# An adaLN transformer block in split float32 on one core: order of the first statistics, rotations, feed-forward rows and last products

## The chip, the core and the metric

One core of a Trainium2 chip. The metric is the device time of one execution in microseconds. The kernel before takes 795.87 us (median of 3 runs, 794.94 to 796.75).

## The reference, cut to what matters

Two batches of 512 tokens of width 512 go through attention with 32 query heads on 8 key heads (rotary embedding, causal mask) and then a gated feed-forward. Both are modulated by six vectors per batch, made from c by one product.

```python
mod = (_silu(L0_c) @ L0_wmod).reshape(L0_c.shape[0], 6, 1, -1)
sa, ca, ga, sb, cb, gb = (mod[:, 0], mod[:, 1], mod[:, 2], mod[:, 3], mod[:, 4], mod[:, 5])
ga = (2 * (ga >= 0) - 1) * jnp.maximum(jnp.abs(ga), 0.25)
gb = (2 * (gb >= 0) - 1) * jnp.maximum(jnp.abs(gb), 0.25)
h = _layernorm(x, axis=-1) * (1 + ca) + sa
x = x + ga * _L0_attn_ref(h, L0_attn_wq, L0_attn_wk, L0_attn_wv, L0_attn_wo)
h = _layernorm(x, axis=-1) * (1 + cb) + sb
x = x + gb * _L0_ffn_ref(h, L0_ffn_w12, L0_ffn_b12, L0_ffn_w3, L0_ffn_b3)
```

In the attention q, k and v are projections of h, q and k are rotated (`q * cos + rotate_half(q) * sin`), and the masked softmax of their product weighs v. The feed-forward is `silu(x1) * x2` of one projection, then a second projection.

## The kernel before, in words

Every float32 product on TensorE is made of three products of rounded parts: each operand has a high part (rounded to fp32r, made by ACT, `split_hi`, L1162) and a low part (operand minus high part, made mostly by POOL, `split_lo`, L1412). A product of 128x512 over 512 rows is thus twelve matmuls.

Five instruction streams are written out by hand, one for each engine, and meet only through semaphores. Each engine takes its stream in order, so a wait holds all that stands behind it. SP issues the DMAs.

*Prologue.* The first batch's rows are normalised on DVE: `bn_stats` (L1064), `norm_scale` (Newton steps, L1011), four `tensor_scalar` (L1067, `x_normed[0]`). PE turns them (`turn_x`), ACT modulates them (`modulate_x`, L1228), DVE and ACT make high and low parts (L1073, L1075, `h_lo[0]`). PE makes k, the four heads q of the first group, v, and between them `modulation_rows(3)` and `(4)` (eight matmuls each). A projection is rotated by `first_rotation(n)` on DVE (three `tensor_tensor`, L823 to L825, `roped`), summed by `rotated_sum` on POOL (L1438, `rope_sum`), split by `rotated_high` on ACT (`rope_hi`) and `rotated_low` on POOL (`rope_lo`). rope_tmp has two buffers, so rotation n waits for `rope_lo` n - 1. In between stand the second batch's statistics (L1087), its `norm_scale(1, 2)`, ACT's normalisation (L1360), `turn_x(1)`, `modulate_x(1, k)` and DVE's `h_low(k)`. POOL waits for `norm_ready` before rotation 1's sum. The first scores need `rope_lo` 5 and `h_ready[1]`.

*Groups.* Eight groups g of eight slots s follow, a slot being one tile of 128 query rows of one batch (r = s % 4; tile order 0, 3, 1, 2) for the four heads of a key head. In a slot PE makes scores (into four `s_bank`s), the next query head (`slot_query`, q_bank), at r = 0 the next k and at r = 2 v (x_bank), the product with v of slot s - 3 (`attend`, o_bank) and the output product of slot s - 4 (`project_out`, out_bank). DVE takes maxima, ACT exponents and normalises, DVE turns 32x32 blocks (`turn_blocks`, L878), SP writes these to DRAM (`blocks_to_dram`, L342) and reads them back by keys (`blocks_to_keys`, L350). ACT and POOL split them in slot s + 2. POOL also splits weights: wq in slots 1 to 4 of a group, wk in slot 2, wv in slot 4, wo in slot 4.

Twelve feed-forward row blocks u (`F_SLOTS`, L41: slots 7, 11, 15, ... 51, r = 3) are prepared beside: loaded in the slot before (`load_f_rows`, which waits for the stores of u - 1, u = 0 for the gates' stores), turned on DVE at the end of slot m (`turn_f`, L1041), split in slot m + 1 (`f_high`, `f_low`), stored in slot m + 2 with eight DMAs of 64 KB (`store_f_rows`, L398). In SP's stream the store of a slot stands behind its load_f_rows, its weight loads and before blocks_to_keys.

*End.* The feed-forward follows: `up` (L785), `gate_up` on DVE, x4 split into `x4_lo`, `down` (L798). `finish(1)` (DVE) gates each row tile i of the second batch (L1147) and adds tiles 0 and 3 (L1152), POOL adds tiles 1 and 2 (`join_y`, L1519). Then the rows are stored.

## Time and profile before

| | |
|---|---|
| median of 3 runs | 795.87 us |
| the profiled execution | 795.66 us, span 793.9 us |
| mean granted TensorE clock | 0.99 of full speed |
| PE busy | 765.9 us (96%) |
| DVE busy | 604.0 us (76%) |
| POOL busy | 567.8 us (72%) |
| ACT busy | 507.3 us (64%) |
| DMA, main queue | 65.1% of 16 engines |

The page shows busy time by engine, the span in 40 slices, the chain of work that ended last, and groups of instructions by line. Times in the trace count from the span's start. The profiled execution is 1.8 us longer than its span: the part outside the first and last instruction. L12 is line 12 of the kernel. An arrow names the releaser of a wait. PEld is the weight load beside PE. Matmuls overlap: twelve of 0.39 us take 2.72 us.

### The profile page before, as it was taken

The page shows a single profiled execution, that of the slowest core. Times are in us where ns is not written, and L with a number is a line of the kernel's source. Part 1 is how long each engine was busy: PE and PEld are TensorE (multiplying, and loading weights), DVE is VectorE, ACT ScalarE, POOL GpSimd, SP SyncE. Part 2 cuts the span into 40 slices and gives each one's busy share as a digit, 9 for nine tenths or more (in the row PEclk, how much of TensorE's full clock was granted, in tenths as well). Part 3 has the DMA queues.
Part 4 walks back from the last instruction along what each step waited for, and adds up shares of the span by engine and source line. Part 5 has one row for each costly group of instructions (what it writes and reads, how often), then busy time and mean ns, then how long its engine had stood idle before and what let it go on. Part 6 is the DMA issues. An engine that isn't in the chain of part 4 may idle for free.

```text
span 793.9 us, 11522 instructions
## 1 busy us (share of the span) xinstructions
PE 765.9 (96%) x3526; PEld 623.4 (79%) x3526; DVE 604.0 (76%) x1296; ACT 507.3 (64%) x1201; POOL 567.8 (72%) x384
## 2 busy tenths in 40 slices
PE   7999999999999999999999999999999998889997
PEld 2755788887888788887888888888888877667885
DVE  5777878777877787778778786868787788459685
ACT  2466775776676766786677666767677765865331
POOL 2545885879587957795779677898768998447453
PEclk9999999999999999999999999999999999999999
DMA  9625646874867576867776767866677855989011
GB/s 314 232 66 143 204 132 186 193 248 117 238 154 234 157 218 154 219 185 199 182 212 190 192 186 189 251 158 211 145 228 188 280 146 170 272 264 248 1 54 53
DMA packets 189781, 147.13 MB, mean 185 GB/s; under 512 B 60564, under 2 KB 166164, under 8 KB 187672
## 3 DMA queue, kind: packets, MB, share of 16 engines
q1 hardware_dynamic: 189304, 146.33, 65.1%
q8 instruction: 28, 0.46, 0.2%
q14 instruction: 33, 0.27, 0.1%
q10 hardware_dynamic: 416, 0.07, 0.0%
HBM read 91.82 MB, written 54.53 MB: 184 GB/s over the span
## 4 chain that ended last, share of the span: by engine, by line
PE 50%; POOL 22%; DVE 11%; ACT 10%; issue 4%; DMA 3%; SPq 1%; DVEq 0%; ACTq 0%; POOLq 0%
PE q_bank L511 12%; PE out_bank L599 11%; POOL pT_lo L1412 7%; PE o_bank L576 7%; PE x_bank L511 7%; PE s_bank L511 5%; POOL rope_tmp L1438 4%; ACT probs L1185 3%; POOL qT L1412 3%; POOL wo_lo_sb L1412 3%; ACT probs L1193 2%; POOL wq_lo_sb L1412 2%; PE s_bank L798 1%; PE s_bank L785 1%; DVE x_y L1134 1%
## 5 line engine op out<-in xcount | busy, mean ns | idle before, releaser
L1412 POOL TENSOR_TENSOR pT_lo<-pT_raw,pT_hi 128x1024 fp32r<-128x1024 f32 (+1 forms) x96 | 194.2, 2038 | 60.1 <-ACT pT_hi L1162 60.1
L1185 ACT ACTIVATE probs<-probs,neg_max 128x32 f32<-128x32 f32 (+15 forms) x256 | 130.6, 512 | 144.8 <-DVE neg_max L860 144.8
L1412 POOL TENSOR_TENSOR qT<-rope_tmp,qT 128x512 fp32r<-128x512 f32 x64 | 83.7, 1308 | 85.4 <-ACT qT L1162 85.4
L878 DVE STREAM_TRANSPOSE turned<-probs 128x512 f32<-128x512 f32 (+1 forms) x64 | 96.7, 1511 | 36.3 <-DMA spread_dram<-turned 28.3
L1438 POOL TENSOR_TENSOR rope_tmp<-rope_tmp 128x512 f32<-128x512 f32 x80 | 110.4, 1388 | 13.2 <-DVE rope_tmp L825 9.4
L1193 ACT ACTIVATE probs<-probs,row_inv 128x32 f32<-128x32 f32 (+15 forms) x256 | 111.9, 508 | 1.8 <-DVE row_inv L868 1.8
L511 PE MATMUL s_bank<-k_both,qT 128*128 128x416 f32 (+11 forms) x576 | 100.6, 324 | 2.0 <-DVE neg_max L860 2.0
L511 PE MATMUL q_bank<-hT_hi,wq_hi_sb 128*128 128x512 f32 x244 | 97.2, 399 | 5.1 <-DVE rope_tmp L825 5.1
L860 DVE CUSTOM_DVE_ANT_0 probs<-s_bank,mask_sb 128x416 f32<-128x416 f32 (+2 forms) x192 | 87.0, 501 | 15.9 <-PE s_bank L511 15.7
L511 PEld LDWEIGHTS s_bank<-k_both,qT 128*128 128x128 f32 x576 | 90.4, 191 | 9.9 <-DVE neg_max L860 2.6
L599 PE MATMUL out_bank<-wo_hi_sb,attn_hi 128*128 128x512 f32 x248 | 97.0, 391 | 1.2 <-DVE attn_lo L882 1.2
L599 PE MATMUL out_bank<-wo_hi_sb,attn_lo 128*128 128x512 f32 x248 | 96.7, 390 | 0.0
L511 PE MATMUL q_bank<-hT_lo,wq_hi_sb 128*128 128x512 f32 x244 | 96.3, 395 | 0.0
L511 PE MATMUL q_bank<-hT_hi,wq_lo_sb 128*128 128x512 f32 x244 | 96.2, 394 | 0.0
L599 PE MATMUL out_bank<-wo_lo_sb,attn_hi 128*128 128x512 f32 x248 | 89.7, 392 | 0.9 <-POOL wo_lo_sb L1412 0.8
L1162 ACT ACTIVATE pT_hi<-pT_raw 128x1024 fp32r<-128x1024 f32 (+1 forms) x96 | 83.6, 903 | 3.9 <-DMA pT_raw<-spread_dram 3.9
L823 DVE TENSOR_TENSOR rope_tmp<-q_bank,cos_sb 128x512 f32<-128x512 f32 x61 | 41.7, 683 | 48.9 <-POOL qT L1412 36.7
L1412 POOL TENSOR_TENSOR wq_lo_sb<-wq_raw,wq_hi_sb 128x512 fp32r<-128x512 f32 x40 | 52.1, 1305 | 20.2 <-ACT wq_hi_sb L1162 20.2
L576 PE MATMUL o_bank<-pT_hi,v_hi 128*128 128x512 f32 x160 | 62.6, 392 | 3.4 <-DVE attn_lo L882 3.4
L576 PE MATMUL o_bank<-pT_hi,v_lo 128*128 128x512 f32 x160 | 62.3, 390 | 0.0
L1162 ACT ACTIVATE qT<-rope_tmp 128x512 fp32r<-128x512 f32 x64 | 39.9, 623 | 33.1 <-POOL rope_tmp L1438 32.4
L511 PEld LDWEIGHTS q_bank<-hT_hi,wq_hi_sb 128*128 128x128 f32 x244 | 46.1, 189 | 15.7 <-DVE rope_tmp L825 6.3
(267 smaller groups left out, 1673.2 us busy)
## 6 DMA issues: line engine op xcount, KB each, us to landing
spread_dram<-turned SPq DMA_DIRECT2D x64, 256.0 KB, 3.8
pT_raw<-spread_dram SPq DMA_DIRECT2D x16, 1024.0 KB, 5.8
spread_dram<-turned SPq DMA_DIRECT2D x64, 192.0 KB, 4.0
pT_raw<-spread_dram SPq DMA_DIRECT2D x16, 768.0 KB, 4.9
wq_raw<-in_L_attn_wq_dram SPq DMA_DIRECT2D x36, 256.0 KB, 4.2
wo_raw<-in_L_attn_wo_dram SPq DMA_DIRECT2D x9, 1024.0 KB, 5.4
spread_dram<-turned SPq DMA_DIRECT2D x64, 128.0 KB, 4.4
pT_raw<-spread_dram SPq DMA_DIRECT2D x16, 512.0 KB, 5.5
```

The lines of the kernel that those rows point to most:

```text
L511: last = pe.matmul(dst, lhs(a, cc), rhs(b, cc), start=(k == 0), stop=(k == len(todo) - 1))
L576: last = pe.matmul(o_bank[:, :], v_s[a][:, b, st_, :], pT[bb][par][:, :, PLACES[par] - 1 - i + st_, :], start=(st_ == 0 and a == 0 and bb ...
L599: last = pe.matmul(dst[:, :], attn[a][:, s % 2, h * P:(h + 1) * P], wo_s[bb][:, h, :], start=(n == 0), stop=(n == len(todo) - 1))
L785: last = pe.matmul(up_banks[u][half][:, :], w12_block(a, k, KC * half + m), h2T[bb][b][:, k, :], start=(n == 0), stop=(n == len(todo) - 1))
L823: nc.vector.tensor_tensor(a, src[:, :], cos_sb[:, :], ALU.mult)
L860: nc.vector.tensor_tensor_reduce(rows, s_banks[t][:, 0:n].rearrange("p (j s) -> p j s", s=W32), mask, -SCALE, HIGHEST, ALU.add, ALU.min, n ...
L878: nc.vector.transpose(dst, src).then_inc(blocks_turned, 1)
L1162: nc.scalar.activation(dst, src, ACT.Copy).then_inc(done, 1)
L1185: nc.scalar.activation(rows, rows, ACT.Exp, bias=neg_max[:, par, t:t + 1], scale=-1.0, accum_out=row_sum[:, par, t:t + 1]).then_inc(exp_do ...
L1193: last = nc.scalar.activation(rows, rows, ACT.Copy, scale=row_inv[:, par, t:t + 1])
L1412: nc.gpsimd.tensor_tensor(dst, src, hi.bitcast(f32), ALU.subtract).then_inc(done, 1)
L1438: nc.gpsimd.tensor_tensor(a, a, b, ALU.add).then_inc(rope_sum, 1)
```

## The change

Five edits, none of which changes what is computed.

- *Prologue, DVE and ACT:* the second batch's statistics and scale stand before all rotations, and ACT normalises before its first rotated high part. ACT's copy of modulation row 3 goes ahead, and high parts and modulations are interleaved anew.
- *Prologue, POOL:* POOL starts its weight parts only when the first batch is normalised, holds the third and fourth head's behind `h_lo[0]` and wv's behind `norm_ready`. Sums and low parts of the query heads go in pairs.
- *Prologue, PE:* `modulation_rows(3)` goes to `s_banks[3]` and ahead of the third head, `project_v(0)` behind `turn_x(1)`, `modulation_rows(4)` to q_bank.
- *Feed-forward rows:* slots 6, 9, 13, ... 49 (r = 1 but for the first), and SP's store stands first in its slot.
- *End:* the last `down` takes its third and fourth part for row tiles 0 and 1, then both for 2 and 3.

```diff
@@ -38,7 +38,7 @@
 F_ROWS = 3 * KC
-F_SLOTS = [TT * (u + 2) - 1 for u in range(F_ROWS)]
+F_SLOTS = [TT + 2] + [TT * (u + 1) + 1 for u in range(1, F_ROWS)]
@@ -219,7 +219,7 @@
         MODS, TURNED = [0, 1, 3, 4, 5, 2], [0, 1, 3, 4]
-        mod_banks = [q_bank, out_bank, out_bank, q_bank, out_bank, x_bank]
+        mod_banks = [q_bank, out_bank, out_bank, s_banks[3], q_bank, x_bank]
         mod_row = [rope_tmp[0:B, 0, 0, :], rope_tmp[0:B, 0, 1, :], f_raw[0:B, :], f_raw[0:B, :], f_blocks[0:B, :], f_blocks[0:B, :]]
@@ -415,6 +415,8 @@
                     v = m // TT + 2
+                    if f_row_at(g, s - 2) is not None:
+                        store_f_rows(f_row_at(g, s - 2))
                     if f_row_at(g, s + 1) is not None:
@@ -448,8 +450,6 @@
                             load_gate(1, b)
-                    if f_row_at(g, s - 2) is not None:
-                        store_f_rows(f_row_at(g, s - 2))
                     if not (first and s == 0):
@@ -605,9 +605,9 @@
                     if first and s == 0:
-
                         turn_rows(3)
                         turn_rows(4)
+                        pe.wait_ge(roped, 5)
                         project_q(out_bank[:, :], 1, 0, h_lo[1])
@@ -677,6 +677,9 @@
                         pe.wait_ge(h_ready[0], k + 1)
+                    if b == 1 and k == KC - 1:
+
+                        pe.wait_ge(mod_rows_copied, 3)
                     for i in range(TT):
@@ -727,9 +730,7 @@
             project_q(out_bank[:, :], 0, 1)
-            pe.wait_ge(wv_lo, 1)
-            pe.wait_ge(roped, 1)
-            project_v(0)
+            modulation_rows(3)
             pe.wait_ge(roped, 2)
@@ -738,9 +739,9 @@
             turn_x(1, range(KC))
+            pe.wait_ge(wv_lo, 1)
+            project_v(0)
             pe.wait_ge(roped, 4)
-            modulation_rows(3)
-            pe.wait_ge(roped, 5)
             modulation_rows(4)
@@ -786,13 +787,13 @@
-            def down(b, parts):
+            def down(b, parts, rows=range(TT)):
                 for ms in parts:
 ...
                         pe.wait_ge(x4_made, 3)
-                    for i in range(TT):
+                    for i in rows:
                         for m in ms:
@@ -807,7 +808,10 @@
                 up(1, m)
-            down(1, ([0, 1], [2], [3]))
+            down(1, ([0, 1],))
+            down(1, ([2],), range(2))
+            down(1, ([3],), range(2))
+            down(1, ([2, 3],), range(2, TT))
@@ -1080,16 +1084,13 @@
-            dve.wait_ge(tables_in, 32)
-            first_rotation(0)
             dve.wait_ge(x_in[2], 16)
             for w in range(TT, 2 * TT):
                 nc.vector.bn_stats(stats[:, w, :], acc[:, w, :]).then_inc(stats_made, 1)
-            first_rotation(1)
             norm_scale(1, 2)
-            first_rotation(2)
-            first_rotation(3)
-            first_rotation(4)
+            dve.wait_ge(tables_in, 32)
+            for n in range(ROPE_FIRST - 1):
+                first_rotation(n)
             for k in range(KC):
@@ -1353,20 +1354,20 @@
             wv_high(0)
-            rotated_high(0, 0, kT[0][0][:, :])
-            rotated_high(0, 1, qT[0][0][:, :, 0, :])
             act.wait_ge(norm_ready, 2)
 ...
                                      scale=rstd[:, w, :]).then_inc(x_normed[1], 1)
-            rotated_high(0, 2, qT[0][0][:, :, 1, :])
+            rotated_high(0, 0, kT[0][0][:, :])
+            copy_rows(3)
+            for h in range(2):
+                rotated_high(0, 1 + h, qT[0][0][:, :, h, :])
             modulate_x(1, 0)
+            rotated_high(0, 3, qT[0][0][:, :, 2, :])
             modulate_x(1, 1)
-            rotated_high(0, 3, qT[0][0][:, :, 2, :])
             modulate_x(1, 2)
+            rotated_high(0, 4, qT[0][0][:, :, 3, :])
             modulate_x(1, 3)
-            rotated_high(0, 4, qT[0][0][:, :, 3, :])
-            copy_rows(3)
             copy_rows(4)
@@ -1531,17 +1532,23 @@
+
+            pool.wait_ge(x_normed[0], TT)
             wk_low(0)
-            for h in range(REP):
-                wq_low(0, h)
+            wq_low(0, 0)
+            wq_low(0, 1)
+            pool.wait_ge(h_lo[0], KC)
+            wq_low(0, 2)
+            wq_low(0, 3)
+            pool.wait_ge(norm_ready, 2)
             wv_low(0)
             rotated_sum(0, 0)
             rotated_low(0, 0, kT[0][0][:, :], kT[1][0][:, :])
-
-            pool.wait_ge(norm_ready, 2)
-            for n in range(1, ROPE_FIRST - 1):
+            for n in (1, 3):
                 rotated_sum(0, n)
+                rotated_sum(0, n + 1)
                 q_first(n)
+                q_first(n + 1)
             rotated_sum(0, ROPE_FIRST - 1)
```

## Rows read from the trace of the kernel before

Rows are whole lines of the profile's views; "..." stands where lines are left out.

**Rows 1.** Waits, 92 to 600 us: who for whom, us in total, times, longest

```profile
PE q_bank L511 <- DVE rope_tmp L825: 4.5, 5, 0.9
```

**Rows 2.** Chain that ended last, in order of time, start: start us, us, what

```profile
17.92 3.68 PE s_bank L681 x16
...
27.60 2.47 DVE stats L1087 x4
...
32.10 0.39 DVE moments L1007 x4
...
34.77 0.69 DVE rope_tmp L823
...
49.74 0.27 PE s_bank L555
```

**Rows 3.** The same chain, 56 to 96 us

```profile
87.61 4.60 PE q_bank L511 x12
```

**Rows 4.** Line L1067, 10 to 20 us: durations ns min/median/max, first and last start

```profile
L1067 DVE TENSOR_SCALAR acc<-acc,moments,rstd x4: 540/1482/1496, 13.1 to 16.4; 128x512 f32<-128x512 f32 x4
```

**Rows 5.** Timeline, POOL, 13 to 62 us: start, us, line, tiles, [idle before <-releaser]

```profile
14.74 2.84 POOL L1412 TENSOR_TENSOR wq_lo_sb<-wq_raw,wq_hi_sb 128x512 fp32r<-128x512 f32 x2
```

**Rows 6.** Timeline, DVE, 19 to 62 us

```profile
19.95 0.43 DVE L1073 CAST hT_hi<-probs 128x512 fp32r<-128x512 f32 x1 [2.09 <-ACT probs L1228]
...
22.96 1.29 DVE L1075 TENSOR_TENSOR hT_lo<-probs,hT_hi 128x512 fp32r<-128x512 f32 x2 [0.79 <-ACT hT_hi L1162]
...
43.82 4.65 DVE L1050 TENSOR_TENSOR hT_lo<-turned,hT_hi 128x512 fp32r<-128x512 f32 x4
...
50.14 1.01 DVE L850 TENSOR_TENSOR probs<-s_bank,mask_sb 128x32 f32<-128x32 f32 x4 [0.47 <-PE s_bank L557]
```

**Rows 7.** Timeline, ACT, 22 to 62 us

```profile
36.80 2.92 ACT L1360 ACTIVATE acc<-acc,shift,rstd 128x512 f32<-128x512 f32 x4
...
45.00 0.76 ACT L1228 ACTIVATE turned<-s_bank,mod,one_plus 128x512 f32<-128x512 f32 x1
```

**Rows 8.** Stretches: us, busy PE/PEld/DVE/ACT/POOL, granted clock, DMA share, GB/s

```profile
14.00:17.90 3.90, 0.81 (x9) 0.64 (x8) 3.86 (x3) 1.51 (x5) 3.58 (x3) 0.86 1.10 352
...
17.90:21.20 3.30, 3.28 (x16) 3.28 (x17) 1.22 (x3) 1.98 (x3) 0.00 (x0) 0.50 1.09 348
...
169.00:171.00 2.00, 2.00 (x15) 1.80 (x14) 1.87 (x2) 1.68 (x3) 2.00 (x1) 1.00 0.15 42
...
187.00:191.00 4.00, 4.00 (x19) 3.31 (x18) 0.98 (x4) 4.00 (x10) 4.00 (x4) 1.00 0.48 84
```

**Rows 9.** Timeline, POOL, 160 to 240 us

```profile
186.07 1.30 POOL L1412 TENSOR_TENSOR f_lo_sb<-f_blocks,f_hi_sb 128x512 fp32r<-128x512 f32 x1
...
189.83 1.30 POOL L1412 TENSOR_TENSOR qT<-rope_tmp,qT 128x512 fp32r<-128x512 f32 x1
...
208.55 1.29 POOL L1412 TENSOR_TENSOR qT<-rope_tmp,qT 128x512 fp32r<-128x512 f32 x1 [5.01 <-ACT qT L1162]
```

**Rows 10.** Timeline, ACT, 160 to 240 us

```profile
188.18 0.62 ACT L1162 ACTIVATE qT<-rope_tmp 128x512 fp32r<-128x512 f32 x1
```

**Rows 11.** Timeline, DVE, 160 to 240 us

```profile
180.41 0.71 DVE L878 STREAM_TRANSPOSE turned<-probs 128x512 f32<-128x512 f32 x1 [0.79 <-DMA spread_dram<-turned]
```

**Rows 12.** Timeline, SP's DMA queue, 150 to 240 us

```profile
187.40 1.93 SPq L398 DMA_DIRECT2D f_dram<-f_hi_sb  x4
...
189.37 2.13 SPq L398 DMA_DIRECT2D f_dram<-f_lo_sb  x4
```

**Rows 13.** Chain in order of time, 735 us to the end

```profile
785.69 0.69 PE q_bank L798 x3
...
789.61 1.66 DVE acc L1152
```

**Rows 14.** Timeline, POOL, 777 us to the end

```profile
781.90 1.29 POOL L1412 TENSOR_TENSOR wq_lo_sb<-wq_raw,wq_hi_sb 128x512 fp32r<-128x512 f32 x1 [3.81 <-ACT wq_hi_sb L1162]
...
787.85 2.87 POOL L1519 TENSOR_TENSOR acc<-acc,y_tmp 128x512 f32<-128x512 f32 x2 [4.66 <-DVE y_tmp L1147]
```

## The prediction, made before the change was run

> **What bounds the kernel now.** I read the page's slices first: PE is busy in nearly all of them, so a change pays only where PE idles or where something else ends last. The waits between 92 and 600 us give one kind of PE stall: q_bank behind DVE's rotation, five times, at most 0.9 us each [rows 1]. The chain in order of time gives the two other places. At the start it runs through DVE, ACT and POOL up to the first scores at 49.74 [rows 2], and goes on through them until PE takes over at 87.61 with twelve products of 4.60 us [rows 3]. At the end it leaves PE at 786.4 and closes with a DVE addition of 1.66 us [rows 13]; the output's transfer follows to 793.9. The change touches all three places. What it does between them is hidden behind PE, as long as covers hold.
>
> **The start, step by step.** (1) Normalising the first batch is four DVE instructions. The fastest, before POOL had begun, took 540 ns, the others 1482 to 1496 [rows 4], while POOL ran weight subtractions of 1.42 us each [rows 5]. With POOL held back until x_normed, all four should take 0.54: from 13.1 to 15.3, and the transposes start at 15.3 rather than 17.92 [rows 2]. Gain 2.6 us.
> (2) DVE ended the first batch's low parts at 24.25 (22.96 + 1.29) [rows 6], 6.3 us after the transposes began; now 21.6 at best. But POOL's wk and the first two wq subtractions, 3 x 1.3 to 1.42 us, now run from 15.3 to about 19.5, and DVE's casts begin 2.0 us after the transposes (19.95 against 17.92), at 17.3. A cast alone is 0.43, a low part 0.65 to 0.69 [rows 6]; beside POOL a low part took 1.16 (4.65 / 4) [rows 6] and a one-input instruction 1.48 [rows 4]. Two such instructions meet POOL: 0 to 1.5 us, I take 0.6. DVE is free at 22.2.
> The Trainium skill ("SBUF — State Buffer", Who interferes with whom) says that GpSimd and VectorE lock one shared port pair for a whole instruction, and that a two-port cast and an instruction with two SBUF inputs both meet it. By this rule the conflict is moved from the normalisation to the casts, and could cost all of the 1.5; the trace agrees with 1482 ns against 540.
> (3) Statistics (2.47) and Newton steps (32.10 to 34.77, 2.67) [rows 2] now follow at once: the second batch's scale is there at 22.2 + 5.15 = 27.35 rather than 34.8.
> (4) From there to the first maxima. Rotation 0: 2.1 (three of 0.69 and gaps), sum 1.3, ACT's high 0.7, low 1.3: 5.4. Rotation 2 waits for that buffer: 2.15, sum 1.35, low of head 0 1.3: 10.2. Rotation 3: 2.15, sum 1.3, high 0.65: 14.3. ACT then has two pairs of modulation and high part at 1.35 [rows 7], one high part, the last pair: 19.0. DVE's low part 0.7, turn of v 0.7, memsets 0.5, and 0.25 of issue: 21.15. The first maxima come at 48.5, before at 50.14 [rows 6]: 1.6 us earlier, of 7.4 that the scale gained. The rest is lost since the rotations, which used to be half done, now all stand behind the scale. ACT's normalisation (2.92) [rows 7] and wv's low part hide beside rotation 0.
> (5) PE has less to wait for: its first scores can start near 46.5. But in group 0 the chain up to 87.61 is DVE's and ACT's, so 1.6 us arrive there and PE idles for the difference. PE idle has a price of its own: the granted clock was 0.50 (1.2 GHz) from 17.9 to 21.2 after little work in 14 to 17.9, [rows 8], and after the gaps before 87.61 twelve products took 4.60 us [rows 3] where three take 0.69 [rows 13]. Unknown, from -1.9 to +1.9 us; I take 0.
> Costed at nothing: modulation 3 on a scores bank (the same 3.6 us on PE, among products that wait for nothing, its weights being requested 10 us before; 3.6 more if they came late), project_v behind the transposes (its reader, the turn of v, comes 5 us later), the two roped waits, three waits on POOL. The new wait on x_normed delays wk_lo to 16.6, before its reader.
> Start: 1.6 us, bounds -0.5 (conflict of 1.5 and 0.6 more on ACT) and 3.5 (no conflict, PE's clock kept up).
>
> **The feed-forward rows.** Each of twelve rows costs DVE 0.6, ACT 0.5, POOL 1.26 and nine issues on SP. All move by about two slots, so the r = 0 slot loses its POOL share. There POOL is busy without a break: f_lo at 186.07, then wq, wv, and the query's low part at 189.83 [rows 9], for which DVE's rotation and then PE waited. Without f_lo this low part could start at 188.57, but ACT's high part, 188.18 to 188.80 [rows 10], holds it to 188.85: 0.97 earlier, more than the stall of 0.9. In its new slot POOL had 5.0 us idle [rows 9]; DVE's turn (0.6) makes the maxima behind it that much later, in a slot where PE has no stall.
> SP is the other side. The eight stores take 1.93 + 2.13 = 4.06 us to issue [rows 12]. They now stand in r = 3, ahead of the weight loads, blocks_to_keys and blocks_to_dram. In slot 3 they fit the time in which SP waited for wo_made; wq and wv go out 4.1 later, and their readers stand in the next slot. In slot 7 blocks_to_keys goes up to 4.1 later, and its reader stands two slots on. But the transfers of slot 3 are queued: DVE's turn at 180.41 was released by one, after 0.79 us idle [rows 11], and from it maxima, exponents and that high part follow without slack. The stores add about 1.9 us of DMA work (0.48 of 4 us) [rows 8]; the queue had a hole of 1.7 us in 169 to 171 (share 0.15) and 0.6 just before, but wq and wv, 1.4 us of work, now fall into the hole. A delay d of that turn gives a stall of about d. Bounds 0 and 2.7, I take 0.4: each stall falls by 0.5, and 5 x 0.5 = 2.5 us. Bounds 4.9 and -9.
> The first row's load comes a slot earlier and waits for the gates' store; blocks_to_keys behind it waits as long for its own blocks.
>
> **The end.** PE's work is the same to 788.4. Before, the last four rows' ends lay 0.68 apart [rows 13], so DVE was behind (its last gating ended at 789.6) and the last addition, 1.66 instead of 0.68, waited for POOL's two, which ran to 790.72 [rows 14]. By pairs the ends are 785.0, 785.7, 787.05 and 788.4. POOL's first addition starts at 786.5, its second at 787.85, ending at 789.2 to 789.5. DVE gates at 788.5 and adds at 789.2: end at 789.9 to 790.3 against 791.27. Gain 1.2 us, bounds 0.9 and 1.5. The fourth part of x4, needed at 785.69 before, must be there at 784.33; POOL has it at 783.2 [rows 14], and if it were late only that stall would be lost.
>
> **Sum.** 1.6 + 2.5 + 1.2 = 5.3 us off the profiled execution's 795.66: 790.36. It stands 0.21 below the median of 795.87, so 790.6.
>
> **Rivals.** (A) The start gains more: casts escape the conflict, and PE, fed from 15.3 on, keeps 2.4 GHz where it had 1.2. For it: the clock fell only at 16.9, after little work. Against: in the end the DVE chain decides. 1.9 at the start more, and d = 0, 2.0 more: 786.7. The Trainium skill ("TensorE: Matmul & The Clock Gate", HAM oscillation) says that idle gaps throttle the array; by this rule filling the gap helps, and the idle before 87.6 hurts. The trace shows both states [rows 8].
> (B) The start gains nothing: conflict and pairwise sums eat 1.6 (sum of head 1 is held until rotation 2, low part 1 behind it). Then 792.2.
> (C) Stalls stay, the stores' transfers move the turn by d = 0.9: 793.1. With B, 794.7.
> (D) Slower: the stores stand ahead of slot 3's transfers, and the hole doesn't take them. It decides from d = 1.8 on, where 5 x 0.9 of loss undo start and end and more. At d = 2.7, five groups lose 1.8 each: 9 us, so 802.1. For it: a turn already released by DMA; against: 2.3 us of hole and the fact that the r = 1 slot gets rid of the same stores.
> (E) The edit of the end doesn't bring what it says, since POOL still overlaps: part of the forecast's width.
>
> **How the numbers follow.** Forecast 0.48 (788 to 793), A 0.15, B 0.13, C 0.12, B with C 0.04, D 0.08. A measurement of this kernel tells about 0.2%, 1.6 us, from no change. Faster by more than that: forecast, A, B and half of C, 0.82; within: the rest of C, B with C, 0.10; slower: D, 0.08. The range leaves out D and the outer part of A: 785.8 to 795.6.
>
> **What would show it.** L1067 at 540 ns four times and transposes near 15.3 (step 1). Casts at L1073 above 1 us (step 2). First maxima near 48.5 and PE's q_bank near 86.0 (steps 4, 5). The five stalls down to about 0.4 us and DVE's wait on spread_dram in slot 4 of a group longer by 0.4 (rows). The last addition at 0.7 to 1.1 us (end). Wrong would be: maxima(0) no earlier, stalls above 1 us, or new PE waits in slots 0, 1 or 7.

## The result and the profile after

The changed kernel takes 803.0 us (799.75 to 806.6, 9 runs) beside 796.7 us of the kernel before in the same session: ratio 1.0087, 95% interval 1.0063 to 1.0111. It is slower by 6.3 us, where 790.6 was forecast. Its profiled execution took 804.21 us, with a span of 802.4.

| | before | after | foreseen |
|---|---|---|---|
| median, us | 796.7 | 803.0 | 790.6 |
| profiled execution / span | 795.66 / 793.9 | 804.21 / 802.4 | 790.4 |
| first maxima on DVE | 50.14 | 48.27 | 48.5 |
| the twelve q_bank products begin | 87.61 | 85.33 | 86.0 |
| PE's last product to DVE's last end | 2.9 | 1.5 | 1.7 |
| PE busy in 92 to 640 us | 542.7 | 538.4 | more |

The start and the end did what was foreseen. The loss lies between them, in the feed-forward rows.

**The start.** DVE's timeline of the changed kernel, 12 to 49 us (start, us, line, tiles, idle before and its releaser):

```profile
12.95 1.91 DVE L1071 TENSOR_SCALAR acc<-acc,moments,rstd 128x512 f32<-128x512 f32 x4
...
16.56 1.16 DVE L1077 CAST hT_hi<-probs 128x512 fp32r<-128x512 f32 x1 [1.70 <-ACT probs L1229]
17.75 1.65 DVE L1079 TENSOR_TENSOR hT_lo<-probs,hT_hi 128x512 fp32r<-128x512 f32 x1
...
21.59 2.46 DVE L1089 BATCH_NORM_STATS2 stats<-acc 128x6 f32<-128x512 f32 x4
...
48.27 0.62 DVE L854 TENSOR_TENSOR probs<-s_bank,mask_sb 128x32 f32<-128x32 f32 x4
```

The normalisation takes 1.91 us for four instead of 4.75, the bulk of which were 1482 to 1496 ns each [rows 4]. The conflict with POOL has moved to one cast and one low part: 1.16 and 1.65 us where [rows 6] shows 0.43 and 0.69 without POOL.

PE's transposes, which start at 15.0 instead of 17.9, take 1.97 us for sixteen instead of 3.68 [rows 2]: the granted clock was 1.00 there, where it was 0.50 before [rows 8]. It then fell to 0.50 all the same, from about 20.7 to 24 us.

**The end.** The chain in order of time, from 796 us:

```profile
796.92 1.37 PE o_bank L799 x6
...
798.32 0.70 DVE y_tmp L1148
...
799.04 0.77 DVE acc L1153
```

The last addition takes 0.77 us instead of 1.66 [rows 13], and DVE ends 1.5 us behind PE (799.81 - 798.29) instead of 2.9.

**The rows.** Waits of the changed kernel between 92 and 640 us (who for whom, us in total, times, longest):

```profile
PE q_bank L511 <- DVE rope_tmp L829: 0.2, 1, 0.2
...
PE out_bank L599 <- ACT wo_hi_sb L1163: 3.8, 4, 2.1
PE out_bank L599 <- DVE acc L910: 2.8, 2, 1.5
PE out_bank L599 <- POOL wo_lo_sb L1413: 2.2, 4, 0.6
...
ACT wo_hi_sb L1163 <- DMA wo_raw<-in_L_attn_wo_dram: 18.5, 6, 4.8
DVE turned L882 <- DMA spread_dram<-turned: 30.5, 20, 6.5
...
SPq L334 <- PE out_bank L599: 1.4, 1, 1.4
```

The five stalls of q_bank [rows 1] are gone. In their place PE waits at out_bank for wo, which ACT gets late from a transfer: six times, up to 4.8 us. DVE, which makes a part of wo's low parts, waits behind ACT, and its maxima and additions stand behind that:

```profile
DVE wo_lo_sb L900 <- ACT wo_hi_sb L1163: 27.5, 6, 6.3
```

In the kernel before this wait is 7.1 us in 7 times. SP's queue in slot 3 of one group shows where the lateness is from (start, us from issue to issue end):

```profile
330.65 3.76 SPq L398 DMA_DIRECT2D f_dram<-f_hi_sb  x4
334.46 2.13 SPq L398 DMA_DIRECT2D f_dram<-f_lo_sb  x4
336.63 0.49 SPq L325 DMA_DIRECT2D wq_raw<-in_L_attn_wq_dram  x1
337.17 0.52 SPq L331 DMA_DIRECT2D wv_raw<-in_L_attn_wv_dram  x1
338.03 0.37 SPq L334 DMA_DIRECT2D wo_raw<-in_L_attn_wo_dram  x1
```

And the chain of the same stretch, with what ACT and PE did at its end (timelines, idle in brackets):

```profile
338.03 8.42 DMA wo_raw<-in_L_attn_wo_dram
```

```profile
346.47 2.19 ACT L1163 ACTIVATE wo_hi_sb<-wo_raw 128x512 fp32r<-128x512 f32 x4 [4.84 <-DMA wo_raw<-in_L_attn_wo_dram]
...
347.24 0.47 PE L599 MATMUL out_bank<-wo_hi_sb,attn_hi 128*128 128x512 f32 x1 [2.12 <-ACT wo_hi_sb L1163]
```

Read it upwards: PE's product waits 2.12 us for ACT, ACT 4.84 us for the load of wo, which takes 8.42 us, and was issued at 338.03, behind wq and wv and eight stores of 5.9 us. In the kernel before the same load went out at 334.51 and ACT used it at 340.66 without a wait. Its median time from issue to landing is 7.8 us, before 5.4 (the rows of DMA issues, KB each, us to landing):

```profile
wo_raw<-in_L_attn_wo_dram SPq DMA_DIRECT2D x9, 1024.0 KB, 7.8
```

Behind this stall PE is slower too. The stretch 347 to 352 us (us, busy PE, PEld, DVE, ACT, POOL, granted clock, DMA share, GB/s):

```profile
347.00:352.00 5.00, 4.76 (x14) 3.42 (x15) 3.81 (x5) 5.00 (x12) 4.30 (x3) 0.66 0.54 184
```

The granted clock is 0.66, a mean of the two levels 2.4 and 1.2 GHz, after PE had been busy for 5.12 of the 7 us before. It is the only stretch between 92 and 640 us in which this trace shows a lower clock; it costs 1.7 us (5 x 0.34).

### The profile page after: what moved, and what is told of

The parts are those of the page before. It is cut to its first block, busy times and chain, and to the rows that moved or that the text cites. A ratio compares the mean times of both kernels' runs of the same rounds, so it can differ in the third digit from the quotient of the medians.

```text
span 802.4 us, 11524 instructions
## 1 busy us (share of the span) xinstructions
PE 772.1 (96%) x3526; PEld 620.0 (77%) x3526; DVE 601.1 (75%) x1296; ACT 507.0 (63%) x1201; POOL 564.0 (70%) x384
## 4 chain that ended last, share of the span: by engine, by line
PE 22%; DVE 21%; DMA 18%; SPq 15%; ACT 11%; issue 6%; POOL 6%; DVEq 0%; POOLq 0%; ACTq 0%
DMA spread_dram<-turned 10%; DMA wo_raw<-in_L_attn_wo_dram 6%; ACT probs L1186 6%; DVE turned L882 5%; SPq L398 5%; SPq L342 5%; PE q_bank L511 4%; PE out_bank L599 4%; SPq L385 3%; DVE rope_tmp L829 2%; PE o_bank L576 2%; PE x_bank L511 2%; POOL qT L1413 2%; DVE rope_tmp L828 2%; PE s_bank L511 2%
## 5 line engine op out<-in xcount | busy, mean ns | idle before, releaser
L1439 POOL TENSOR_TENSOR rope_tmp<-rope_tmp 128x512 f32<-128x512 f32 x80 | 107.9, 1355 | 15.4 <-DVE rope_tmp L829 15.4
L599 PE MATMUL out_bank<-wo_hi_sb,attn_hi 128*128 128x512 f32 x248 | 99.4, 401 | 8.6 <-ACT wo_hi_sb L1163 3.8
L599 PE MATMUL out_bank<-wo_lo_sb,attn_hi 128*128 128x512 f32 x248 | 91.5, 398 | 2.5 <-POOL wo_lo_sb L1413 2.5
L599 PEld LDWEIGHTS out_bank<-wo_hi_sb,attn_hi 128*128 128x128 f32 x248 | 47.1, 190 | 24.8 <-issue 11.7
```

The source lines that it names most:

```text
L599: last = pe.matmul(dst[:, :], attn[a][:, s % 2, h * P:(h + 1) * P], wo_s[bb][:, h, :], start=(n == 0), stop=(n == len(todo) - 1))
L1439: nc.gpsimd.tensor_tensor(a, a, b, ALU.add).then_inc(rope_sum, 1)
```

## The experiments

Each edit stands against the kernel named. The base from the second group on is *store_last* (787.9 us). Ratios are to the kernel before in the same session (795.2 to 796.0 us), with their 95% interval. *store_last* was not measured again in the later sessions, so a difference of under 0.8 us to it is not read. Each version has one trace.

### The rows undone, and the rows alone

*rows_undone*: the changed kernel with slots and store as before.

```diff
-F_SLOTS = [TT + 2] + [TT * (u + 1) + 1 for u in range(1, F_ROWS)]
+F_SLOTS = [TT * (u + 2) - 1 for u in range(F_ROWS)]
...
-                    if f_row_at(g, s - 2) is not None:
-                        store_f_rows(f_row_at(g, s - 2))
                     if f_row_at(g, s + 1) is not None:
...
+                    if f_row_at(g, s - 2) is not None:
+                        store_f_rows(f_row_at(g, s - 2))
                     if not (first and s == 0):
                         blocks_to_keys(g, s - 1)
```

> The changed kernel with the feed-forward rows and SP's store back in their old places; prologue and end stay changed. Theory W (the whole loss comes from the row stores, which in slot 3 of a group stand ahead of wo's load; ACT's wo_high then waits for the load, and PE's output product behind it): 796.7 - 2.3 at the start (q_bank at 85.3 instead of 87.6) - 1.2 at the end = 793.2, and PE's five stalls of 0.9 us behind the rotation are back. Rival P (the prologue, by putting the engines out of phase, causes part of the loss): 797 or more.

Measured: 792.81 us (791.59 to 793.23), ratio 0.9961 (0.9949 to 0.9974). The stalls are back (q_bank 4.5, 5 times, 1.0), the waits at out_bank are down to 0.8 us. The edits of start and end are worth 3.0 us, as theory W had it (793.2 expected).

*rows_alone*: the reverse, the kernel before with the changed slots and the changed place of the store.

> The kernel before with only the feed-forward rows moved (slots and SP's store first in the slot). Theory W: the changed kernel's 803.0 plus the 3.5 us that prologue and end no longer give: 806.5. Rival P (part of the loss needs the new prologue): 800 or less, with ACT waiting for wo_raw under 5 us in total.

Measured: 807.44 us (804.08 to 809.26), ratio 1.0143 (1.0122 to 1.0164). ACT's wait for wo_raw 18.8 us, wo's flight 7.8. The rows alone cost 11.7 us on the kernel before, and 10.2 (803.0 - 792.8) on the changed one: the loss doesn't need the new prologue, and rival P is refuted.

### Where in the slot the stores stand

The slots stay those of the change; only the eight stores of slots 3 and 7 are moved. *store_before_wo* puts them behind the loads of wq and wv, *store_behind_wo* behind wo's, *store_behind_keys* behind those of keys and v, *store_last* behind the slot's own writes. The diff of *store_last*, with the places of the others marked in it:

```diff
                     v = m // TT + 2
-                    if f_row_at(g, s - 2) is not None:
+                    both = f_row_at(g, s - 2) is not None and f_row_at(g, s + 1) is not None
+                    if both:
                         store_f_rows(f_row_at(g, s - 2))
...
                             load_wv(UNITS[v][0])
+                    # the two lines here in store_before_wo
                     if r == 3 and fresh(m // TT):
                         sp.wait_ge(wo_made, m - 3)
                         load_wo(UNITS[m // TT][0])
...
+                    # here in store_behind_wo
                     if not (first and s == 0):
                         blocks_to_keys(g, s - 1)
...
+                    # here in store_behind_keys
                     blocks_to_dram(g, s)
                     if makes_v(g, s):
                         store_v(g, 2 + s // TT)
...
                         sp.dma_start(gates_dram[a, :, :], mod_row[(2, 5)[a]]).then_inc(gates_out, 16)
+                    if f_row_at(g, s - 2) is not None and not both:
+                        store_f_rows(f_row_at(g, s - 2))
```

(Row 0, whose store and next load fall into one slot, stays first.)

> As the changed kernel, but the eight stores stand behind the loads of wq and wv and ahead of wo's load (in slot 7, where no wo is loaded, they stay first). Theory W (wo's load is issued behind the stores, its reader in slot 4 waits, and nothing else of the order matters): wo is as late as in the changed kernel, so the same 802 to 804 us, ACT's wait for wo_raw near 18 us. Rival Q (whatever lies behind the stores is late because their 4096 packets of 128 bytes are still being worked off): also late, but with wq and wv out earlier the same 802 to 806. Rival V (wq and wv, issued together with wo behind the stores, share the DMA engines with wo and make its flight 7.8 instead of 5.5 us): flight falls to 6.5 and the time to about 797.

> The changed kernel, but SP's store stands behind the weight loads and wo's load, ahead of blocks_to_keys (in slot 8, where the next row is loaded in the same slot, it stays first). Theory W: wo's load goes out as before and lands in some 5.3 us, the wait of ACT for it is gone; 790 to 793. Rival Q (the loss comes from the transfers of slot 3's blocks being delayed by the stores in the queue, whatever stands first): these are delayed as much or more, so 800 or above, with DVE's wait on spread_dram in slot 4 of each group at 2 us or more.

> The changed kernel, with the eight stores of slots 3 and 7 behind the loads of weights, wo, keys and v, and ahead of the slot's own writes to spread_dram. Theory W2 (every transfer that stands behind the stores and has a reader with little slack pays; here these are the four writes, the copy to keys that waits for them, and DVE's turned, which waits for its buffer): wo_raw on time, DVE's wait for spread_dram above 40 us, 800 to 820 us. Rival L (only loads pay, since their readers stand in the next slot, while the writes have a whole slot): 787 to 790.

> The changed kernel, but SP's store stands at the end of its slot, behind blocks_to_dram (slot 8 as before). Neither wo's load nor slot 3's blocks have the stores ahead of them. Theories W and Q both: 790 to 792; a difference between this run and the store behind wo's load is the price of the stores ahead of the blocks. Rival P: 797 or more.

| stores stand | us (runs' range) | ratio (interval) | ACT for wo_raw, us | DVE's turned for spread_dram, us | PE for DVE's acc, us |
|---|---|---|---|---|---|
| first (the change) | 803.0 (799.75 to 806.6) | 1.0087 (1.0063 to 1.0111) | 18.5 | 30.5 | 2.8 |
| before wo | 798.7 (797.7 to 799.1) | 1.0037 (1.0025 to 1.0048) | 14.6 | 28.0 | none shown |
| behind wo | 815.8 (812.6 to 816.4) | 1.0244 (1.0224 to 1.0264) | none shown | 56.6 | 14.7 |
| behind keys | 819.0 (817.2 to 821.8) | 1.0293 (1.0271 to 1.0315) | none shown | 62.2 | 15.2 |
| last | 787.9 (787.2 to 788.2) | 0.990 (0.9884 to 0.9915) | none shown | 15.0 | 0.3 |

Five places, five prices from 0 to 31 us for the same eight transfers. Whatever stands behind them pays. Ahead of wo it is wo. Behind wo it is the copy to keys and the slot's four writes, and that is dearer: DVE's next turned can't begin before these writes have landed, since it fills the same buffer. A part of these two prices is TensorE's clock: between 92 and 640 us the granted clock fell in three stretches in each of the two traces, worth 5.2 and 5.1 us, against one worth 1.7 in the change and none in *store_last* (each slice of 4 us times what its clock lacks to 1.00). SP's queue of *store_behind_wo* and of *store_last*, same slot, in this order:

```profile
340.76 0.37 SPq L334 DMA_DIRECT2D wo_raw<-in_L_attn_wo_dram  x1
341.17 2.46 SPq L398 DMA_DIRECT2D f_dram<-f_hi_sb  x4
343.68 3.95 SPq L398 DMA_DIRECT2D f_dram<-f_lo_sb  x4
347.74 0.53 SPq L350 DMA_DIRECT2D pT_raw<-spread_dram  x1
...
349.04 2.76 SPq L342 DMA_DIRECT2D spread_dram<-turned  x4
```

```profile
330.65 0.37 SPq L334 DMA_DIRECT2D wo_raw<-in_L_attn_wo_dram  x1
331.38 0.52 SPq L350 DMA_DIRECT2D pT_raw<-spread_dram  x1
...
332.69 2.42 SPq L342 DMA_DIRECT2D spread_dram<-turned  x4
335.17 4.45 SPq L398 DMA_DIRECT2D f_dram<-f_hi_sb  x4
339.66 2.96 SPq L398 DMA_DIRECT2D f_dram<-f_lo_sb  x4
344.25 0.36 SPq L378 DMA_DIRECT2D f_raw<-in_L_ffn_w_dram  x1
344.72 0.52 SPq L350 DMA_DIRECT2D pT_raw<-spread_dram  x1
```

In the first, the writes go out 8.3 us after wo's load (349.04 - 340.76); in the second 2.0 us after it, and the stores' 7.4 us of issue fall into a stretch in which SP has little else to send. Between 92 and 640 us PE is then busy for 547.0 of 548 us, against 542.7 before and 538.4 after. The copy to keys itself goes out 14.1 us after wo's load, in *rows_undone* 10.4: 3.7 us later, and PE doesn't wait for it.

*store_behind_wo* refutes my first theory, that only wo's load matters: it expected 790 to 793. Rival Q's condition came (800 or above, DVE's wait for spread_dram at 2 us or more: 5.4 at the longest). *store_behind_keys* refutes that only loads pay. *store_before_wo* came in below what theory W and rival Q expected (802 and more), and near rival V: wo's flight is 6.4 us instead of 7.8, and the time 798.7 where V said about 797. So some 4 us of the loss, and 1.4 of wo's flight, go away when wq and wv stand ahead of the stores instead of between them and wo. *store_last* is 2 us better than the 790 to 792 that all theories expected.

The version with the stores last beats both kernels: 4.95 us under the version without the row edits. That is what the five stalls were worth; the prediction's bound was 4.9. Counted the same way over 13 to 93 us, the clock costs both versions 3.4 us, so the difference is not from there.

### Issue time or packets?

The eight stores hold SP for 4.2 to 5.9 us and put 4096 packets of 128 bytes in the queue. On *store_last*, two dummies stand at the place where the change has its stores. *dummy_issue*: eight issues, next to no bytes. *dummy_work*: two issues with all the packets. Both add transfers whose data nobody reads.

```diff
...
+                        for a in range(2 * QT):
+                            sp.dma_start(scratch[f_row_at(g, s - 2), 0, a, 0:1, :],
+                                         mask_sb[0:1, 0:W32]).then_inc(dummy_out, 16)
```

```diff
...
+                        for a in range(2):
+                            sp.dma_start(scratch[f_row_at(g, s - 2), a, :, :, :].rearrange("c p m -> p c m"),
+                                         mask_sb[:, :].rearrange("p (c m) -> p c m", m=W32)).then_inc(dummy_out, 16)
```

> On the version with the stores last in their slot (787.9 us): at the head of those slots, where the changed kernel issues its stores, SP issues eight transfers of 128 bytes each from a constant to a scratch tensor. They cost SP issue time (0.35 to 0.5 us each, 3 to 4 us in all) and next to no DMA work. Theory I (SP's issue time delays wo's load past its slack of about 0.8 to 2 us): wo's load goes out 2 to 3 us late, ACT waits for wo_raw, 794 to 800 us. Rival P (it is the 4096 small packets, not the issue): at most 1 us slower, 788 to 789.

> On the version with the stores last in their slot (787.9 us): at the head of those slots two transfers from a constant to a scratch tensor with the stores' whole DMA work, 4096 packets of 128 bytes, 512 KB, but two issues instead of eight. Theory I (issue time): SP is held for about 1 us, time within 1.5 us of 787.9. Rival P (the small packets ahead in the queue): flight of wo's load 7 to 8 instead of 5.5 us, DVE's wait for spread_dram above 20 us, 793 to 800 us.

Measured: issue 787.87 us (787.05 to 790.84), packets 793.05 (791.81 to 795.54). SP's queue in one group of *dummy_issue*, then of *dummy_work*:

```profile
325.99 2.37 SPq L424 DMA_DIRECT2D scratch_dram<-mask_sb  x8
...
330.45 0.37 SPq L336 DMA_DIRECT2D wo_raw<-in_L_attn_wo_dram  x1
```

```profile
327.19 3.81 SPq L424 DMA_DIRECT2D scratch_dram<-mask_sb  x2
...
332.26 0.53 SPq L333 DMA_DIRECT2D wv_raw<-in_L_attn_wv_dram  x1
332.84 0.51 SPq L336 DMA_DIRECT2D wo_raw<-in_L_attn_wo_dram  x1
```

2.4 us of issue cost nothing in the median, and theory I (794 to 800) is refuted. They shorten SP's wait for the release of wo's buffer, which lasts 22.5 us in 7 times in *store_last* and 7.2 in 7 here; wo goes out at 330.45, as at 330.65 in *store_last*. A small price can't be excluded: the six runs spread over 3.8 us. The traced one took 789.79 us, had ACT waiting for wo_raw for 2.7 us in 2 times, and its granted clock stayed at 1.00 over the start, where the clock costs *store_last* 3.4 us.

The two issues with the packets cost 5.2 us. SP still waited for wo's buffer in five of seven groups, so that wo's load went out on time there; the fence shows one of the two in which it didn't. What the packets change is above all the flight: wo's load takes 7.5 us to land instead of 5.5, and ACT waits for it 9.4 us in 6 times, of which 4.6 in groups where the load was on time and 4.8 in the two others (DVE's turned for spread_dram 18.8 us, not above 20 as expected). Two issues can also take as long as eight: the first line of the second fence is 3.81 us for two, in other groups 1.43; what makes the difference isn't shown. So of the 15.1 us between stores first and stores last, 5.2 are shown to come from two issues with the packets. The rest has the packets and an issue of 4.2 to 5.9 us together, more than the 3.2 us that SP waited for wo's buffer; an issue of that length without packets was not run, so that share isn't separated further.

The Trainium skill ("DMA: Bandwidth & Descriptors", Queues, rings and completion order) says that on each DMA engine a queue's descriptors are consumed in ring order. By that a load behind 4096 small packets isn't begun before them; the 5.5 and 7.5 us agree, but they don't tell waiting in the queue from sharing the engines.

### Old slots with the stores last

*old_slots_store_last* is *rows_undone* with the store at the end of its slot, r = 1:

```diff
-                    if f_row_at(g, s - 2) is not None:
-                        store_f_rows(f_row_at(g, s - 2))
                     if not (first and s == 0):
                         blocks_to_keys(g, s - 1)
...
                         sp.dma_start(gates_dram[a, :, :], mod_row[(2, 5)[a]]).then_inc(gates_out, 16)
+                    if f_row_at(g, s - 2) is not None:
+                        store_f_rows(f_row_at(g, s - 2))
```

> The changed kernel with the rows in the slots of the kernel before (7, 11, ...), their store at the end of the slot in which it stood (slot r = 1) instead of ahead of blocks_to_keys. It separates what the version with the stores last gained by the place of the stores from what it gained by the slots. Theory F (the five stalls come from f_lo standing on POOL ahead of wq, wv and the query's low part in slot r = 0, so only the slots take them away): the stalls of 4.5, 5 and 1 us remain, 791.5 to 793.5 us, as the 792.8 with the old order. Rival S (the stalls come from where the stores stand): they shrink, 788 to 790 us.

Measured: 830.87 us (829.19 to 833.13), ratio 1.0443 (1.0427 to 1.046). Neither theory's time: 38 us worse than the same slots with the store ahead of the keys. But PE's stalls at q_bank behind the rotation stay, 5.5 us in 6 times, as theory F said: it is the slots that take them away, not the place of the stores. SP's waits between 92 and 640 us name a candidate, a load that waits for the stores to have landed:

```profile
SPq L378 <- DMA f_dram<-f_lo_sb: 17.7, 11, 3.5
```

It is the next row's load, and with the old slots it stands at the head of the slot right behind the stores, ahead of wq and the keys. *old_late_load* moves it to the end of its slot:

```diff
-                    if f_row_at(g, s + 1) is not None:
-                        load_f_rows(f_row_at(g, s + 1))
                     if fresh(v):
...
                     if f_row_at(g, s - 2) is not None:
                         store_f_rows(f_row_at(g, s - 2))
+                    if f_row_at(g, s + 1) is not None:
+                        load_f_rows(f_row_at(g, s + 1))
```

> The version with the old slots and the stores at the end of their slot (830.9 us), but the load of the next row, which waits for the stores' completion (17.7 us of SP's waiting in 11 times), is moved from the head of the next slot to its end, behind the slot's writes. Theory H (that wait at the head of the slot holds wq, keys and writes, and is the cause of the 38 us): 791.5 to 796. Rival O (in slot r = 1 the stores' issue and transfers themselves are in the way of slot 2's keys, whatever SP waits for): 815 or more.

Measured: 801.4 us (799.67 to 803.88), ratio 1.0074 (1.0053 to 1.0096). Moving the wait from the head was worth 29.5 of the 38 us, so theory H has the main cause, though the time lies outside its range and outside rival O's. 8.6 us remain, and their cause is open; wo's load takes 7.2 us instead of 5.5 here too, and the stalls at q_bank are again there (5.2 us in 5 times). In *store_last* SP has the same wait, also 17.7 us in 11 times, and it costs nothing: it falls at the head of slots 0 and 4, where the copy to keys can go out those 3.7 us later.

### Start and end, one at a time

All on *store_last*, 787.86 us. *end_undone* takes the last products in their old order:

```diff
-            down(1, ([0, 1],))
-            down(1, ([2],), range(2))
-            down(1, ([3],), range(2))
-            down(1, ([2, 3],), range(2, TT))
+            down(1, ([0, 1], [2], [3]))
```

> The version with the stores last in their slot (787.9 us), with the last products of batch 1 by parts of x4 as before, not by row pairs. Theory (the pairs shorten the tail behind PE's last product from 2.9 to 1.5 us): 1.2 to 1.5 us slower, 789.2, the last DVE addition 1.6 us instead of 0.77. Rival (POOL's additions overlap all the same): within 0.4 us of 787.9.

Measured: 789.21 us (788.61 to 789.82), 1.35 slower, the last addition 1.66 us.

*start_undone* reverses the change's edits of the start on all engines (PE's order and mod_banks, DVE, ACT, POOL), of which these are the core:

```diff
-            dve.wait_ge(x_in[2], 16)
+            dve.wait_ge(tables_in, 32)
+            first_rotation(0)
+            dve.wait_ge(x_in[2], 16)
...
-            pool.wait_ge(x_normed[0], TT)
             wk_low(0)
-            wq_low(0, 0)
-            wq_low(0, 1)
-            pool.wait_ge(h_lo[0], KC)
-            wq_low(0, 2)
-            wq_low(0, 3)
-            pool.wait_ge(norm_ready, 2)
+            for h in range(REP):
+                wq_low(0, h)
             wv_low(0)
```

> The version with the stores last in their slot, with the whole start as in the kernel before: order on PE, DVE, ACT and POOL, banks of the modulation rows. Theory (the 2.3 us that the start gained at PE's products of q_bank at 85.3 arrive at the end): 790.2, first maxima near 50.1, q_bank near 87.6. Rival (later slots take the gain back): within 0.5 us of 787.9.

Measured: 789.62 us (789.01 to 790.92), 1.8 slower. Its trace has the first maxima at 49.24 and the twelve products at 86.69, 1.0 and 0.95 us later than *store_last* (48.25 and 85.74), not the 2.3 expected. The kernel before has the same order and is 0.9 us later still (50.14, 87.61), already at rotation 0, which waits for PE's k (25.47 against 24.57). PE's granted clock was 0.50 from about 17 to 23 us there, and in *start_undone* only from about 18 to 21.5. So some 0.9 of the 2.3 us goes with the clock, for the order of work is the same in these two.

*pool_free* drops two of POOL's new waits:

```diff
-            pool.wait_ge(x_normed[0], TT)
             wk_low(0)
...
-            pool.wait_ge(h_lo[0], KC)
             wq_low(0, 2)
```

> The version with the stores last, without POOL's two waits at the start (for the first batch's x_normed and h_lo): POOL subtracts the weights as soon as they are there. Step 1 of the prediction (the conflict costs the normalisation 2.8 us): its four instructions again 1.48 us, transposes at 17.9 instead of 15.1, first maxima 1.5 to 2.8 us later, 789.4 to 790.5. Rival (the conflict has only moved to the casts, and what the normalisation loses they win back): low parts done within 0.8 us of 21.6, time within 0.6 of 787.9.

Measured: 790.47 us (788.39 to 790.72), 2.6 slower; first maxima at 50.81 instead of 48.25. Its DVE timeline:

```profile
13.09 4.76 DVE L1074 TENSOR_SCALAR acc<-acc,moments,rstd 128x512 f32<-128x512 f32 x4
19.93 0.43 DVE L1080 CAST hT_hi<-probs 128x512 fp32r<-128x512 f32 x1 [2.08 <-ACT probs L1232]
20.39 0.69 DVE L1082 TENSOR_TENSOR hT_lo<-probs,hT_hi 128x512 fp32r<-128x512 f32 x1
...
24.15 2.46 DVE L1092 BATCH_NORM_STATS2 stats<-acc 128x6 f32<-128x512 f32 x4
```

The casts are quick, but all begins 3 us later, and the statistics at 24.15 instead of 21.60. Holding POOL back is worth more than the conflict that it moves.

*pool_held* holds POOL back longer:

```diff
             wk_low(0)
+            pool.wait_ge(h_lo[0], KC)
             wq_low(0, 0)
             wq_low(0, 1)
-            pool.wait_ge(h_lo[0], KC)
```

> The version with the stores last (787.9 us), with POOL's wait for the first batch's low parts moved ahead of the first two subtractions of wq instead of the last two. Theory (the subtractions of wq beside the casts cost DVE 1.08 instead of 0.43 and 1.65 instead of 0.69 us): cast and low part at 0.43 and 0.69, the low parts done near 20.4 instead of 21.6, first maxima 0.8 to 1.2 us earlier, 786.7 to 787.2. Rival (the chain at the start then waits for ACT's high parts or for wq's low parts on POOL, which are 4 us later): within 0.5 us of 787.9, or up to 1.5 slower.

Measured: 788.47 us (787.4 to 789.18), 0.6 slower than the base, not told apart from it and as the rival expected. DVE, with the normalisation beginning at 13.46 in this execution, 0.5 later than in the base:

```profile
17.09 0.43 DVE L1080 CAST hT_hi<-probs 128x512 fp32r<-128x512 f32 x1 [1.72 <-ACT probs L1232]
17.55 0.69 DVE L1082 TENSOR_TENSOR hT_lo<-probs,hT_hi 128x512 fp32r<-128x512 f32 x1
...
20.83 2.46 DVE L1092 BATCH_NORM_STATS2 stats<-acc 128x6 f32<-128x512 f32 x4
...
23.75 1.04 DVE L1022 TENSOR_SCALAR var_eps<-moments 128x4 f32<-128x4 f32 x1
24.82 1.21 DVE L1023 TENSOR_SCALAR rstd<-var_eps 128x4 int32<-128x4 int32 x1
```

The conflict is gone from the casts and comes back in two instructions of four elements per partition, 1.04 and 1.21 us where the base has 0.17 each: 1.9 us, more than the 1.27 won until then. The Trainium skill ("SBUF — State Buffer", Who interferes with whom) says that the engine that comes second is held for the other's whole instruction; these rows agree, for a tiny instruction takes nearly as long as one subtraction of POOL beside it, 1.28 us.

The first maxima come at 49.41, 1.2 later than in the base (0.5 of it from the later start), where they were expected earlier. Yet this execution took 787.4 us, the fastest of its six. Its twelve products at q_bank begin at 86.47, 0.7 later than the base's, but take 2.85 us instead of 4.61. The stretch 84 to 90 us in *store_last*, then in *pool_held*:

```profile
84.00:90.00 6.00, 5.37 (x20) 4.37 (x21) 5.94 (x10) 5.42 (x10) 4.85 (x4) 0.72 0.84 245
```

```profile
84.00:90.00 6.00, 4.65 (x24) 3.89 (x24) 5.94 (x9) 6.00 (x11) 4.85 (x4) 1.00 0.84 254
```

The granted clock stayed at 1.00; why it did here isn't shown. Over 13 to 93 us the clock costs the base 3.4 us, this execution nothing, *pool_free* 6.9 and *stats_late*, below, 3.3. That is as much as the differences measured here, and one trace for each version doesn't tell how often it falls. So the differences of 1 to 3 us that the edits of the start make hold for the medians, but what part of them is the order of work and what the clock is open.

*stats_late* puts DVE's first two rotations back around the second batch's statistics:

```diff
+            dve.wait_ge(tables_in, 32)
+            first_rotation(0)
             dve.wait_ge(x_in[2], 16)
...
+            first_rotation(1)
             norm_scale(1, 2)
-            dve.wait_ge(tables_in, 32)
-            for n in range(ROPE_FIRST - 1):
+            for n in range(2, ROPE_FIRST - 1):
```

> The version with the stores last, with DVE's order of the start as before: rotation 0, the second batch's statistics, rotation 1, Newton steps, and the rest. The scale should be there at about 31 instead of 26.8. Step 4 of the prediction (what the early scale gains is mostly lost again, since all rotations stand behind it): first maxima within 1.5 us of 48.3, time 787.9 to 789.4. Rival (the early scale is what the start gains by): first maxima 3 to 4 us later, 790 to 792.

Measured: 792.42 us (791.59 to 793.92), 4.6 slower, first maxima at 52.72. The rival was right. POOL's timeline says why:

```profile
31.95 1.29 POOL L1418 TENSOR_TENSOR wv_lo_sb<-wv_raw,wv_hi_sb 128x512 fp32r<-128x512 f32 x1 [7.60 <-DVE shift L1028]
```

With the change POOL waits for the scale before wv's low part and all sums of rotations. The early statistics are thus needed by the new order of POOL: with it and late statistics the first maxima come later (52.72) than in the kernel before (50.14).

## Why the prediction was wrong, point by point

**Start: right in size, in part by luck.** Forecast 1.6 us; 1.8 by *start_undone*, and 2.3 in the trace at the twelve products, of which some 0.9 go with the clock. Step 1 held (1.91 us for four, transposes at 15.0). Step 2 had two errors that nearly cancel. It took 0.6 us for the conflict, which cost 1.27 (*pool_held* without it against the base). And it took 6.3 us from the transposes to the last low part, a figure from a stretch at a granted clock of 0.50; at 1.00 and without conflict *pool_held* needs 5.4 (15.52 to 20.91). So DVE was free at 21.6, not 22.2. Step 4 gave 48.5 for the first maxima, measured 48.27: the scale was 0.6 us earlier than forecast and the way from it 0.35 longer. Its remark that most of the scale's gain is lost again was misread by me as "the early scale matters little", and *stats_late* showed 4.5 us. Step 5's zero for PE's clock held for the twelve products (4.62 us, before 4.60 [rows 3]), but *pool_held*'s 2.85 shows that the bounds of 1.9 us either way were no exaggeration. Rival B is refuted. Rival A had its sign at the transposes (1.97 us instead of 3.68), but of its 1.9 us at the start no more than 0.7 is there: the clock fell later instead, and the casts didn't escape the conflict.

**End: right.** 1.2 forecast, 1.35 measured. Rival E is refuted.

**Rows: the step that failed.** 2.5 us of gain were forecast, and 10.2 of loss came. The gain's side was even too small: the stalls went wholly, and with the stores out of the way that is 4.95 us. The failed sentence is this: in slot 3 the stores "fit the time in which SP waited for wo_made; wq and wv go out 4.1 later, and their readers stand in the next slot". Three things are wrong with it.
- The load that SP waited for, wo's, is itself behind the stores, and it was given no term. In the group at 334.51 its reader on ACT had 0.75 us to spare (334.51 + 5.4 against 340.66), and the normalisation, the next high parts and DVE's share of wo's low parts stand behind it.
- The issue doesn't fit. The stores' price was 4.06 us [rows 12], but SP's wait for wo's buffer in the kernel before is 21.6 us in 7 times, 1.5 to 4.6 each and above 4.06 in one group only, so that by these figures wo's load goes out about 1 us late (4.06 - 3.1) even at the forecast's own price. In the new place the issue took 4.2 to 5.9 us, and the wait, still 22.7 us in 7 times in *rows_undone*, is 1.4 in 1. *dummy_issue* shows that an issue which fits (2.4 us) costs nothing in the median: the logic was right and the size was not.
- The packets were costed at 1.9 us of DMA work that a hole takes up. *dummy_work* shows 2.0 us more flight for wo's load and 5.2 us of time. wq and wv, "4.1 later", are not free either: ahead of the stores they save some 4 us (*store_before_wo*).

**Rival C** is refuted by the stalls, which are gone. **Rival D** came nearest, at 802.1: slower, because the stores stand ahead of slot 3's transfers. Its number is no confirmation, for it had the delay at DVE's turn. That delay is there too (26.3 us before, 30.5 after, longest 6.5 instead of 2.1), but PE's own waits are at out_bank, most of them behind wo. D had a chance of 0.08, since I asked whether the DMA engines had a hole, and not, for each transfer behind the stores, who reads it and how much time it has.

**The account.** Start and end gave 3.0 us (*rows_undone*). The rows took 10.2: 4.95 won at the stalls, 15.1 lost by the place of the stores (803.0 - 787.9). Together 7.2, against 6.3 measured directly in another session; *rows_alone* has 11.7 for the rows, so the parts don't add up closer than about 1.5 us. In 92 to 640 us the changed kernel does 69 products fewer than *store_last* (2530 against 2599 at 0.21 us each, 14.5 us), which is nearly all of the 15.1. 8.5 us of that are idle time (PE is idle for 9.6 us there, in *store_last* for 1.0). In the other 6 us PE counts as busy, with its products further apart: 1.7 of them are the granted clock of 0.66 behind the one stall, and where the rest goes isn't shown.

## What to carry to other kernels

A transfer that is moved up a queue is paid for by everything that it passes: list each transfer behind it with its reader, and the time between its landing and its use, and include the one whose wait you mean to fill. Put bulk stores that nobody waits for behind the last transfer of the slot that has a reader, and look where the wait for their completion then stands. When a transfer is to fill a wait, compare its price with that wait group by group, not only in kind. When an edit removes a real stall and the kernel still gets slower, try its parts apart: here the slots were worth 5 us, and only the place of the stores in them was wrong.

## What the runs showed of the hardware

- 512 KB in packets of 128 bytes ahead in the same queue lengthened a 1 MB load from 5.5 to 7.5 us, though SP issued the load on time in five of seven groups.
- The time that the same issues take varies: two of 256 KB took 1.43 to 3.81 us, the eight stores 4.1 to 8.8 us.
- DVE instructions of 4 elements per partition took 1.04 and 1.21 us beside a POOL subtraction of 1.28, and 0.17 without.
- The same twelve products took 2.85 us at a granted clock of 1.00 and 4.6 us where it fell to 0.50 among them; sixteen transposes 1.97 and 3.68 us.
